# First self attention of a two-layer block: step 0 loaded from inside the projections, and one head's maxima joined through a positive gap in each second slot

## What is computed

```
h = layernorm(x) * g + b
q, k, v = h @ q1_w, h @ k1_w, h @ v1_w     # 16 heads of 16
s = q @ k.T * 16**-0.5                     # per head, 1024 x 1024
x = x + softmax(s) @ v @ o1_w + o1_b
```

## Time and profile before

| | us |
|---|---|
| median of 3 runs | 4137.87 |
| the runs | 4121.34 to 4141.66 |
| the profiled execution | 4131.29 |
| its span | 4128.5 |

### The profile page before, as it was taken

One profiled execution on the slowest core, in us unless ns is written; L12 is line 12 of the kernel. 1 busy time (PEld: TensorE's weight loads), 2 busy tenths in 40 slices (PEclk: granted clock), 3 DMA queues, 4 the chain that ended last, 5 costly groups with the idle time before them and its releaser, 6 DMA issues. The chain is left out here.

```text
span 4128.5 us, 63035 instructions
## 1 busy us (share of the span) xinstructions
PE 3835.3 (93%) x23695; PEld 2391.4 (58%) x23695; DVE 2710.5 (66%) x4469; ACT 2378.3 (58%) x3310; POOL 1860.5 (45%) x1220
## 2 busy tenths in 40 slices
PE   3799999995998998998999999999999969999899
PEld 2544443433557886885555555555555537777787
DVE  6599999953536754435666676666766547665665
ACT  2477777772443334445777777777777744443332
POOL 1287891001202102005788877878878743222200
PEclk9799999997779999999999999999999989999999
DMA  5745344405622006883222222222222110000100
GB/s 167 179 63 73 61 53 53 44 2 99 106 39 57 19 13 214 313 318 135 82 79 86 77 82 93 78 83 90 80 82 73 47 41 10 3 9 1 43 16 16
DMA packets 314174, 328.16 MB, mean 79 GB/s; under 512 B 129592, under 2 KB 232952, under 8 KB 309520
## 3 DMA queue, kind: packets, MB, share of 16 engines
q1 hardware_dynamic: 311216, 315.17, 28.5%
q0 software_dynamic: 2656, 8.97, 0.8%
HBM read 195.47 MB, written 127.55 MB: 78 GB/s over the span
## 5 line engine op out<-in xcount | busy, mean ns | idle before, releaser
L1840 POOL TENSOR_TENSOR f_sums<-f_sums,f_probs 128x1024 f32<-128x1024 f32 x384 | 917.0, 2388 | 116.8 <-ACT f_probs L1985 78.3
L1859 DVE TENSOR_REDUCE f_mx<-f_s 128x1 f32<-128x512 f32 x992 | 634.9, 682 | 338.7 <-PE f_s L2010 330.9
L1985 ACT ACTIVATE f_probs<-f_st 128x1024 f32<-128x1024 f32 x512 | 520.4, 1016 | 327.9 <-PE f_st L2054 327.7
L1528 ACT ACTIVATE f_probs<-f_st 128x512 f32<-128x512 f32 x1024 | 535.9, 601 | 168.6 <-PE f_st L1586 168.3
L1397 DVE TENSOR_REDUCE f_mx<-f_s 128x1 f32<-128x512 f32 x960 | 599.9, 682 | 29.2 <-PE f_s L1548 6.8
L1953 ACT ACTIVATE f_st<-f_shift 128x1024 f32<-128x1024 f32 x512 | 526.6, 1029 | 23.0 <-DMA f_shift<-shift 6.9
L2070 PE MATMUL f_acc<-f_probs,f_v 128*64 128x512 f32 x2048 | 496.2, 606 | 0.0
L2010 PE MATMUL f_s<-f_k,f_q 64*128 64x512 f32 x2976 | 479.3, 412 | 4.7 <-DVE f_mx L1859 4.7
L2010 PEld LDWEIGHTS f_s<-f_k,f_q 64*128 64x128 f32 x2976 | 268.3, 184 | 245.3 <-DVE f_mx L1859 127.9
L2054 PE MATMUL f_st<-f_q,f_k 64*128 64x512 f32 x3072 | 399.2, 390 | 5.2 <-ACT f_st L1953 5.2
L1586 PE MATMUL f_st<-f_q,f_k 50*128 50x512 f32 x1024 | 333.3, 474 | 6.9 <-ACT f_probs L1528 6.8
(11 more groups left out here) (377 smaller groups left out, 7839.9 us busy)
## 6 DMA issues: line engine op xcount, KB each, us to landing
q<-f_stage SPq DMA_DIRECT2D x80, 512.0 KB, 2.8
k<-f_stage SPq DMA_DIRECT2D x80, 512.0 KB, 2.8
f_q<-q SPq DMA_DIRECT2D x32, 1024.0 KB, 5.0
f_k<-k SPq DMA_DIRECT2D x32, 1024.0 KB, 7.3
f_shift<-shift SPq DMA_DIRECT2D x32, 1024.0 KB, 4.7
v<-f_v_stage SPq DMA_DIRECT2D x64, 256.0 KB, 2.9
f_v<-v SPq DMA_DIRECT2D x32, 512.0 KB, 3.9
f_q<-q SPq DMA_DIRECT2D x96, 128.0 KB, 4.4
```

What stands on the lines that cost most here:

```text
L1528: a_.activation(probs[:, n % NP, e % 2, :], stb[k % 3][:, :], ACT.Exp, scale=L.scale).then_inc(p_ready, 1)
L1840: g_.tensor_tensor(out, out, probs[:, n % NP, :, :], ALU.add).then_inc(sum_done, 1)
L1859: v.tensor_reduce(mx[:, i % 2, c:c + 1], bank[u % 3][:, :], AX_X, ALU.max).then_inc(s_free, 1)
L1985: a_.activation(probs[:, s % NP, :, :], stb[s % 2][:, :, :], ACT.Exp, scale=L.scale).then_inc(p_ready, 1)
```

## The change

1. **Step 0 loaded in the projections.** The operands of set 0 are allocated ahead of both stages. In `norm_project` of block L0, POOL fills k and v of the set with ones after the rstd of tile 2. At tile 3 SP waits for the stores of tiles 0 and 1 and for the ones, and loads v in plain rows of 64 into `v_rows`; behind each q or k store of tiles 3, 4 and 5 it issues one of the 12 loads. POOL spreads `v_rows` into v after its last rstd. In the attention, SP counts the loads of step 0 as done, and TensorE waits for four memsets (sets 1 and 2) instead of six.
2. **Joined slots.** In a slot with j = 1, the first half (f = 0) of row half r = 0 becomes the difference of both halves, by two matmuls, one of them with negated keys (`minus`, made by ScalarE once a step). ScalarE cuts it with Relu into `aside` in SBUF, ahead of the third exponential of that slot. VectorE doesn't reduce this unit; for f = 1 it adds `aside` to the scores and takes the maximum in one instruction (`tensor_tensor_reduce`), which covers both halves. The unit's bank is freed by the copy, so who takes a bank waits for `s_free`, and for `copied` too (`bank_free`).

The diff, cut to its core:

```diff
-    def norm_project(self, L, x_sb, ident, g, b, wq, wk, wv):
+    def norm_project(self, L, x_sb, ident, g, b, wq, wk, wv, step0=None):
...
+                    if step0 and t == 3:
+                        for k in range(ring):
+                            sp.wait_ge(c_out[k], 16 * use * 2)
+                        for k in range(2):
+                            sp.wait_ge(v_out[k], 16 * (vunits // 2) * 2)
+                        sp.wait_ge(ones_set, 2)
+                        sp.dma_start(v_rows[:, :, :], self.v.rearrange("(r d) -> r d", d=gw)[0:N, :]
+                                     .rearrange("(c p) x -> p c x", p=P)).then_inc(v_first, 16)
...
+                            if step0 and 3 <= t < 6:
+                                dst, src = first_rows[(t - 3) * chunks + c]
+                                sp.dma_start(dst, src).then_inc(q_first, 16)
...
+                if step0:
+                    sp.wait_ge(q_first, 16 * 12)
...
                 for t in range(2, TILES):
                     self.norm_rstd(pool, n, t)
+                    if step0 and t == 2:
+                        nc.gpsimd.memset(step0["k"][:, :, :].bitcast(F32), 1.0).then_inc(ones_set, 1)
+                        nc.gpsimd.memset(step0["v"][:, :, :, :], 1.0).then_inc(ones_set, 1)
+                if step0:
+                    pool.wait_ge(ones_set, 2)
+                    pool.wait_ge(v_first, 16)
+                    nc.gpsimd.tensor_copy(step0["v"][:, :, :, 0:L.hd], v_rows[:, :, :].rearrange("p c (h d) -> p c h d", d=L.hd))\
+                        .then_inc(v_spread, 1)
+                    pool.wait_ge(v_spread, 1)
...
+        def joined(slot):
+            return slot % 2 == 1
...
+        taken = [at[u] for u in order if u[0] == "s" and joined(u[2]) and u[3:] == (0, 0)]
+        joins = [at[u] for u in order if u[0] == "s" and joined(u[2]) and u[3:] == (1, 0)]
+        place = {u: n for n, u in enumerate(taken)}
+
+        def copied_to(u):
+            return sum(1 for x in taken if x <= u)
+
+        def vector_to(u):
+            return u + 1 - copied_to(u)
...
+                sp.sem_inc(q_in[0], QLOADS)
+                sp.sem_inc(v_in[0], 16 * KC)
                 sp.wait_ge(set_done, 2)
-                load(0)
-                sp.wait_ge(set_done, 4)
                 load(1)
...
-                for k in slots_of:
+                for k in range(1, DEPTH):
                     g_.memset(k_[k][:, :, :].bitcast(F32), 1.0).then_inc(set_done, 1)
                     g_.memset(vs[k][:, :, :, :], 1.0).then_inc(set_done, 1)
...
                         u = at["s", i, slot, f, r]
+                        if u in place:
+                            continue
                         dve.wait_ge(s_ready, u + 1)
                         c = ((r * 2 + j) * QB + qb) * 2 + f
+                        if joined(slot) and r == 0:
+                            n = place[at["s", i, slot, 0, 0]]
+                            dve.wait_ge(copied, n + 1)
+                            v.tensor_tensor_reduce(larger[:, :], bank[u % 4][:, :], aside[:, n % 2, :], 1.0, -3.0e38, ALU.add, ALU.max,
+                                                   mx[:, i % 2, c - 1:c]).then_inc(s_free, 1)
+                            continue
...
+                def set_aside(i, slot):
+                    u = at["s", i, slot, 0, 0]
+                    n = place[u]
+                    act.wait_ge(s_ready, u + 1)
+                    if n >= 2:
+                        act.wait_ge(s_free, vector_to(joins[n - 2]))
+                    a_.activation(aside[:, n % 2, :], bank[u % 4][:, :], ACT.Relu).then_inc(copied, 1)
+
+                def negate_keys(i):
+                    cur = i % DEPTH
+                    act.wait_ge(q_in[cur], (i // DEPTH + 1) * QLOADS)
+                    if i > 2:
+                        act.wait_ge(s_ready, at["s", i - 2, SLOTS - 1, 0, 0] + 1)
+                    a_.activation(minus[0:SROWS, i % 2, :], k_[cur][0:SROWS, 1, HALF:N], ACT.Copy, scale=-1.0).then_inc(minus_done, 1)
...
                         for e in range(4):
+                            if e == 0 and s == 13 and i + 2 < STEPS:
+                                negate_keys(i + 2)
+                            if e == 2 and held:
+                                set_aside(*held)
...
-                pe.wait_ge(set_done, 6)
+                def bank_free(u):
+                    pe.wait_ge(s_free, vector_to(u - 4))
+                    if copied_to(u - 4):
+                        pe.wait_ge(copied, copied_to(u - 4))
+
+                pe.wait_ge(set_done, 4)
...
-                        pe.wait_ge(s_free, u - 3)
+                        bank_free(u)
+                        gap_here = u in place
+                        if gap_here:
+                            pe.wait_ge(minus_done, i)
+                            t.matmul(bank[u % 4][:, :], q[cur][rows, j, qb * P:(qb + 1) * P], minus[rows, i % 2, :],
+                                     start=True, stop=False, tile_position=(64 * r, 0))
                         t.matmul(bank[u % 4][:, :], q[cur][rows, j, qb * P:(qb + 1) * P], k_[cur][rows, j, f * HALF:(f + 1) * HALF],
-                                 start=True, stop=True, tile_position=(64 * r, 0)).then_inc(s_ready, 1)
+                                 start=not gap_here, stop=True, tile_position=(64 * r, 0)).then_inc(s_ready, 1)
...
```

More of the change, by code:

```diff
@@ L1246, in _, with narrow_rows, attend_narrow @@
                 ring.each(pe, step)
-    def attend_narrow(self, L, x_sb, ident, wo, bo):
+    def narrow_rows(self, L, i, q, k_):
+        G, HD = L.group, L.hd
+        rows = slice(i * G * HD, (i + 1) * G * HD)
+        loads = []
+        for buf, pieces in ((q, (self.q[0], self.q[1], self.q[0])), (k_, (self.k[0], self.k[0], self.k[1]))):
+            for n, src in enumerate(pieces):
+                view = src[rows, :].rearrange("(j r e) t -> r e j t", j=2, r=2)
+                for r in range(2):
+                    row = 64 * r + HD * n
+                    loads.append((buf[row:row + HD, :, :].bitcast(F32), view[r]))
+        return loads
+    def attend_narrow(self, L, x_sb, ident, wo, bo, step0):
         nc = self.nc
@@ L1330, in load @@
                     slot = i % DEPTH
[L1331 to L1337, removed]
+                    for dst, src in self.narrow_rows(L, i, q[slot], k_[slot]):
+                        sp.dma_start(dst, src).then_inc(q_in[slot], 16)
                     view = self.v.rearrange("(r d) -> r d", d=G * HD)[i * N:(i + 1) * N, :].rearrange("(c p) (h d) -> p c h d", p=P, d=HD)
@@ L1611, in rows @@
                     half, u = n % 2, at["rows", n // 2, n % 2]
-                    pe.wait_ge(s_free, at["back", n // 2, half] + 1)
-                    pe.wait_ge(s_free, u - 3)
+                    pe.wait_ge(s_free, vector_to(at["back", n // 2, half]))
+                    bank_free(u)
                     for k in range(4):
@@ L1618, in project @@
                 def project(i, half):
-                    pe.wait_ge(s_free, at["rows", i, half] + 1)
+                    pe.wait_ge(s_free, vector_to(at["rows", i, half]))
                     pe.wait_ge(w_low, 1)
@@ L3595, in build @@
             L, L1 = Layer("L0", 16, 4, None), Layer("L1", 64, 2, None)
-            self.norm_project(L, x_sb, ident, *gains[0], q["q1_w"], q["k1_w"], q["v1_w"])
-            self.attend_narrow(L, x_sb, ident, q["o1_w"], p("o1_b"))
+            with ExitStack() as ahead:
+                step0 = self.first_step(ahead, "n0_", [P, N // P, L.group, L.tile])
+                self.norm_project(L, x_sb, ident, *gains[0], q["q1_w"], q["k1_w"], q["v1_w"], step0)
+                self.attend_narrow(L, x_sb, ident, q["o1_w"], p("o1_b"), step0)
             self.context_kv(L, x_sb, q["k2_w"], q["v2_w"])
```

34 lines of the change are left out of this document (25 added, 9 removed).

## The result

The changed kernel took **4162.2 us** (median of 7 runs, 4155.4 to 4172.6); before, in as many runs on the same chip, 4137.9 (4121.3 to 4144.8). The ratio is 1.0073, with a 95% interval of 1.0054 to 1.0092: **slower by 0.7%**. The forecast was 4158.

A forecast was written before the change was run, and what follows sets the result against it. The prediction took a ring between ScalarE and TensorE, not VectorE, to bound plain slots. Early load -8 and joined slots +35 made +27 on the profiled 4131.3: 4158 us, range 4117 to 4188.

The forecast's parts named there:

- The ring between ScalarE and TensorE: Plain slots of the steady steps: exponentials and matmuls waiting on each other take 2.60 us, so lighter VectorE shortens none.
- Part A: Step 0 loaded in projection tiles 3 to 5: 12.8 us gained at the hand-over, 5 lost to DMA, -8 together.
- Part B: Joined slots, 120 in the steady steps: 29 + 4 + 1.5 + 0.7, +35 us together.
- The bank wait: Back and rows slots: last score waits for the Relu's bank, +0.7 in 29 and +0.63 in 14, +29 us.
- The sum-and-max: VectorE in joined slots: 0.61 us to the next as lower bound, 1.22 as upper; +4 us for late ones.
- The added matmul and late next banks: TensorE: added matmul hidden in plain slots, 0.7 us in y slots; late ones +4 over 74 joined slots.
- Turn: Last reduction of a step ends 0.2 us later in even steps, earlier in odd ones: +1.5 us.
- The rival that VectorE paces: Steady steps: 120 x 0.6 = 72 us come off, 4051, or 4080 with bank waits paid; chance 0.10.
- That the bank wait is covered: Back and rows slots: only the early load and small costs are left, 4129, at best 4118; chance 0.17.
- A dear sum-and-max: Joined slots: the operation costs twice a reduction, +41 us in place of +4, 4195; chance 0.12.
- That A is swallowed: Projections stretch by all that the early load saves, 4166; chance 0.06.
- Its signs: If right: plain slots 2.60, back and rows slots 0.6 to 0.7 longer, a step of 45.5 to 46.5 us.

The follow-up runs named there:

- the last experiment: Changed kernel with the other row half joined, keys negated in slot 11, TensorE's wait for four memsets moved behind the first phase: 4131.3 us, ratio 0.9996.
- the one with v alone: Step 0's v loaded early, its 12 q and k loads issued in the attention as before, no joined slots: 4138.2 us, one run.
- the halved maxima: Kernel before, each steady-step maximum over 256 of 512 columns, exponentials scaled by a sixteenth (another function): 4118.5 us, ratio 0.9966.
- the moved wait: Changed kernel without joined slots, TensorE's wait for four memsets moved from the attention's start to ahead of the first turn: 4118.0 us, ratio 0.996.
- the other row half: Changed kernel with the difference made for row half 1 instead of 0, everything else alike: 4134.4 us, ratio 1.0005.
- the plain joins: Changed kernel with joins in slots 1, 3, 9 and 11 only, none beside back or rows, 60 instead of 120: 4129.1 us, ratio 0.9987.

## Why the prediction was right

- **What bounds.** The ring between ScalarE and TensorE paces plain slots: they stayed at 2.61 with 65 us less on VectorE, and with 255 less.
- **Part A**, -8.0 for -8 in the profiled execution. The wait moved from the loads to the four memsets as forecast, and the 12.8 of gain was right. That the price of 5 fits is in part luck. As a sum it was right where the clock stayed at 1.00 in the tiles with loads (the stage starts 5.4 later here, 5.2 in the last experiment): over the ten traces with the whole early load it starts up to 8.2 later, 6.6 in the middle, and the early load alone brought the first exponential forward by 6.6. Nor was it right in its parts: in the trace of after the three tiles with loads gave 3.0, not 5, and 2.2 came in tiles 0 and 1, before any load. In those two SP issues its third store at 81.6 instead of 79.6, in each kernel with the early load's code, the one with v alone among them, and not in those without (79.9 and 80.3). Why is open; no run was made for it. That TensorE's clock could fall in a tile with loads was in none of the terms.
- **Part B**, +38.1 for +35. The bank wait was the mechanism, and the choice of another bank removed it from back. Its term was undersized: 0.80 and 0.69 in place of 0.70 and 0.63, mostly because the last score goes 0.14 after the Relu's end and not 0.05. Over 29 and 14 slots that is 3.8 us, and B came out 3.1 above the forecast.
- **The sum-and-max**: the lower bound held, 0.61 to the next (0.60 to 0.62 in all 120). The Trainium skill was right in the two instructions. The price that the prediction put on the second, 0.16 from a tiny operation's row, was wrong: it was 0, and the slots behind are 0.05 longer, not 0.15. That 0.05, which the prediction took for late ones, comes from the sum-and-max starting 0.11 later than it had it.
- **The added matmul and late next banks**: +4.2 for +4.7, y at 5.44 and 5.63 included.
- **Turn**: +1.0 for +1.5, with 2.4 in even steps and -1.4 in odd ones. The forecast's reason ("The last reduction ends 0.2 later in even steps, earlier in odd ones") was right (0.3 later, 0.2 earlier), and so was its 0 for the keys, which the profile of after seemed to contradict.
- **The rival that VectorE paces** falls with the halved maxima, where it had 60 us or more and 14 came, and with the changed kernel, where it had 72. That the bank wait is covered falls with back at 3.88. A dear sum-and-max falls with 0.61. That A is swallowed falls with the early load alone; by 0.9982 with its upper end at 1.0001 it is a small gain, not a certain one, while the moved wait makes it certain.
- **Its signs.** Back slots were to be 0.6 to 0.7 longer and a step 45.5 to 46.5; they were 0.80 longer and 46.6 to 46.8, just outside, by the same undersized term. The total came within 4 us because A's term fitted and B's miss was small; what carries the forecast is the mechanism in back and rows.

## What to carry to other kernels

Before an engine is relieved, look for a stage, or a slot, that goes without its work: if it takes as long, the relief is worth only what the special slots wait for. When a buffer of a ring is freed by another engine's later instruction, count who takes units between; the same work with another unit freed cost 27 us less. And where two neighbouring slots change, compare their sum before blaming what stands between them.

## What was not expected of the hardware

The mean granted clock differs from execution to execution of the same program: of the kernel before, among the runs beside the first experiments, one took 4112.9 us at 0.962 and another 4145.5 at 0.953. Where in the program that lies can't be seen for one program, of which one trace is kept, but across the kernels the last step shows it, though no edit touches it. Rows of after, in the last step, and of before in the part of it at the lower level (half, 1.2 GHz):

```profile
938.00:965.30 27.30, 26.25 (x91) 7.33 (x91) 1.37 (x3) 14.91 (x29) 0.00 (x0) 0.50 0.00 1
```

```profile
915.70:922.50 6.80, 6.80 (x27) 2.01 (x27) 0.68 (x2) 3.88 (x8) 0.00 (x0) 0.50 0.00 0
```

At half clock a slot there takes 4.07 instead of 2.61. The last step took 40.9 where none or hardly any of it was at half clock (the joined slots alone, the moved wait, the halved maxima, the other row half, all but the last join, the last experiment), 43.6 before and up to 52.2 in the plain joins, with nothing in common in what had been changed ahead of it. So the 7.5 by which the two profiled executions differ there is no cost of the change: with the same joins, the joined slots alone took 40.9. The rest of the program took from 3183.3 (the early load alone) to 3203.8 (the plain joins), so the 4.7 between before and after is within what unchanged stages differ by. What a change costs was therefore read from the stages that it touches, and from ratios over several runs; a single run's total can't tell 11 us.
